# Folding the output weights over three steps of the attention instead of one, with the routed expert beats moved towards later steps

## The reference

```
q   = rmsnorm(rope(xn @ Wq_c @ Wq_up))            16 heads of 128
ao  = softmax(window scores, 64 keys) @ v + softmax(block scores, 16 blocks) @ ck
out = einsum('btgf,gfi->btgi', ao, Wg).reshape(...) @ Wo      4 groups of 4 heads
ffn = mean of 2 shared experts + sum over the top 6 of 32 routed experts
      of gate * (relu(xn @ w1 + b1) @ w2 + b2)
x   = x + out + ffn
```

## Time and profile before

| | |
|---|---|
| median of 3 runs | 601.38 us (600.21 to 603.71) |
| profiled execution | 597.51 us |
| its span | 595.7 us |
| busy TensorE, VectorE, ScalarE, GpSimd | 526.1, 335.0, 313.2, 328.8 us |
| steps -1 to 8 | from 83 us |

### The profile page before, as it was taken

One profiled execution on the slowest core, in us unless ns is written; L12 is line 12 of the kernel. 1 busy time (PEld: TensorE's weight loads), 2 busy tenths in 40 slices (PEclk: granted clock), 3 DMA queues, 4 the chain that ended last, 5 costly groups with the idle time before them and its releaser, 6 DMA issues.

```text
span 595.7 us, 9656 instructions
## 1 busy us (share of the span) xinstructions
PE 526.1 (88%) x2951; PEld 400.3 (67%) x2951; DVE 335.0 (56%) x884; ACT 313.2 (53%) x739; POOL 328.8 (55%) x235
## 2 busy tenths in 40 slices
PE   0998998799767999999999999999979997899982
PEld 0565786688666777788777887889757454455561
DVE  3479834233074471844818448251565986999654
ACT  1215136364556766767657676575621228667530
POOL 3000448868677685766867768654311024788770
PEclk9799998899899999999999999999999999999998
DMA  9940639778978886575765757865377012456667
GB/s 285 364 166 6 164 88 216 187 154 206 282 173 224 205 215 139 127 157 123 157 163 111 168 129 156 178 147 104 36 240 237 0 33 65 70 95 90 96 91 223
DMA packets 87281, 90.39 MB, mean 152 GB/s; under 512 B 26688, under 2 KB 75264, under 8 KB 86848
## 3 DMA queue, kind: packets, MB, share of 16 engines
q1 hardware_dynamic: 66608, 61.50, 35.4%
q0 software_dynamic: 19584, 27.24, 26.7%
q10 hardware_dynamic: 1040, 1.05, 0.5%
HBM read 65.32 MB, written 22.60 MB: 148 GB/s over the span
## 4 chain that ended last, share of the span: by engine, by line
PE 48%; DVE 16%; issue 12%; DMA 9%; ACT 7%; POOL 7%; SPq 0%; POOLq 0%; ACTq 0%; DVEq 0%
PE bank L559 9%; DMA expert_sums<-expert_weights,token_of_slot 7%; PE bank L896 6%; PE bank L904 3%; PE bank L905 3%; POOL tiles L1098 3%; PE bank L551 2%; PE bank L523 2%; PE bank L1804 2%; DVE sum_squares L686 2%; PE bank L568 2%; PE bank L491 2%; PE bank L511 2%; ACT normed L607 2%; POOL expert_weights L858 2%
## 5 line engine op out<-in xcount | busy, mean ns | idle before, releaser
L866 POOL DMA_INDIRECT expert_sums<-expert_weights,token_of_slot x79 | 128.8, 1631 | 55.2 <-ACT expert_weights L928 37.9
L858 POOL DMA_INDIRECT expert_weights<-normed_x,token_of_slot x79 | 94.5, 1196 | 109.2 <-DVE token_of_slot L366 45.6
L896 PE MATMUL bank<-expert_weights 128*88 128x128 f32 x632 | 85.3, 278 | 0.6 <-ACT expert_weights L921 0.4
L896 PEld LDWEIGHTS bank<-expert_weights 128*88 128x88 f32 x632 | 75.7, 161 | 1.2 <-issue 1.2
L559 PE MATMUL bank<-out_weights,expert_weights 128*128 128x256 f32 x256 | 60.1, 380 | 1.4 <-ACT expert_weights L644 1.4
L928 ACT ACTIVATE expert_weights<-bank,chosen_bf 128x256 f32<-128x256 f32 x79 | 37.7, 477 | 38.1 <-PE bank L905 18.9
L1105 POOL DMA_INDIRECT expert_sums<-expert_weights,token_of_slot x23 | 46.5, 2021 | 13.6 <-issue 5.5
L904 PE MATMUL bank<-expert_weights 88*128 88x256 f32 x158 | 48.6, 389 | 5.6 <-ACT expert_weights L928 5.5
L559 PEld LDWEIGHTS bank<-out_weights,expert_weights 128*128 128x128 f32 x256 | 46.4, 190 | 8.2 <-ACT expert_weights L644 3.1
L719 DVE SCALAR_TENSOR_TENSOR expert_weights<-bank,blocks_valid 128x64 f32<-128x64 f32 x32 | 7.1, 222 | 73.8 <-ACT expert_weights L621 73.8
L905 PE MATMUL bank<-expert_weights 89*128 89x256 f32 x158 | 47.6, 382 | 0.0
(11 more groups left out here) (276 smaller groups left out, 1087.5 us busy)
## 6 DMA issues: line engine op xcount, KB each, us to landing
expert_weights<-experts_out SPq DMA_DIRECT2D x79, 192.8 KB, 2.9
expert_weights<-experts_in SPq DMA_DIRECT2D x79, 176.0 KB, 3.2
expert_weights<-L_ffn_wi SPq DMA_DIRECT2D x32, 128.0 KB
expert_weights<-w_comp SPq DMA_DIRECT2D x1, 2048.0 KB, 9.1
expert_weights<-fold_g SPq DMA_DIRECT2D x1, 2048.0 KB, 13.8
expert_sums<-zeros SPq DMA_DIRECT2D x2, 1024.0 KB, 18.7
expert_weights<-L_ffn_wo SPq DMA_DIRECT2D x16, 128.0 KB
normed<-expert_sums SPq DMA_DIRECT2D x2, 1024.0 KB, 5.7
```

The source lines that it names most:

```text
L858: nc.gpsimd.indirect_dma_start(xt0[g % 4], None, xn0, bass.IndirectOffsetOnAxis(ap=MAP[:, g:g + 1], axis=0)).then_inc(gathered[g % 4], 16)
L866: nc.gpsimd.indirect_dma_start(sums0[g % 2], bass.IndirectOffsetOnAxis(ap=MAP[:, g:g + 1], axis=0), yt0[g % 2], None, compute_op=ALU.add). ...
L896: ins = nc.tensor.matmul(ps[5][0:DHB, c * P:(c + 1) * P], w[:, k * DH + c * DHB:k * DH + (c + 1) * DHB], xT0[g % NXT][:, k * P:(k + 1) * P ...
```

## The change

The tables of beats and folds are new: the beats per slot in steps -1 and 0 are thinned to 4 and 6, in steps 2 to 7 there are two beats in slot s = 0; the eight folds have their places in steps -1 (four), 0 (two) and 1 (two). The transfers of the values of batches 2 and 3 stand four beats earlier in SyncE's loop. The number of beats and folds and the work in each are the same.

```
-BEATS = {g: (1,) * 8 for g in range(FIRST_STEP, NT)}
-BEATS[NT] = (1,) * 7 + (0,)
+BEATS = {-1: (0, 1, 0, 1, 1, 0, 1, 0), 0: (1, 1, 0, 1, 1, 0, 1, 1), 1: (1,) * 8, **{g: (1, 1, 1, 1, 2, 1, 1, 1) for g in range(2, NT)},
+         NT: (1,) * 7 + (0,)}
+FOLDS = {(-1, 1): 0, (-1, 3): 1, (-1, 4): 2, (-1, 6): 3, (0, 4): 4, (0, 6): 5, (1, 4): 6, (1, 6): 7}
...
@@ attention_pe, and the same in attention_act with take_folded
-                if g == 0:
-                    fold(pe, k)
+                if (g, k) in FOLDS:
+                    fold(pe, FOLDS[g, k])
...
-                if g == 0:
-                    fold(pe, NG + s)
+                if (g, NG + s) in FOLDS:
+                    fold(pe, FOLDS[g, NG + s])
...
@@ SyncE's loop over beats
-                    if i == 48:
+                    if i == 44:
                         sp.wait_ge(pv_ps, NWIN)
-                    if 48 <= i < 49 + NWIN:
-                        load_values(sp, 2, i - 48)
-                    if i == 64:
+                    if 44 <= i < 45 + NWIN:
+                        load_values(sp, 2, i - 44)
+                    if i == 60:
                         sp.wait_ge(pv_ps, 2 * NWIN)
...
-                    if 64 <= i < 65 + NWIN:
-                        load_values(sp, 3, i - 64)
+                    if 60 <= i < 61 + NWIN:
+                        load_values(sp, 3, i - 60)
```

More of the change, by code:

```diff
@@ L662, in attention_act @@
                     probs_T(act, g - 2, 0)
-                if g == 0:
-                    take_folded(act, k)
+                if (g, k) in FOLDS:
+                    take_folded(act, FOLDS[g, k])
             for s in range(NSUB):
@@ L671, in attention_act @@
                         probs_T(act, g - 2, s + 1)
-                if g == 0:
-                    take_folded(act, NG + s)
+                if (g, NG + s) in FOLDS:
+                    take_folded(act, FOLDS[g, NG + s])
                 for i in beats(g, NG + s):
```

## The result

Over 19 runs of each the changed kernel takes 606.03 us (603.78 to 609.34) and the kernel before 603.49 (599.78 to 608.23). The ratio is 1.0047, with a 95% interval of 1.0028 to 1.0066: about 2.8 us slower, where 7.4 us faster was forecast. Some 2.9 us of the 8.5 arise ahead of step -1, where both kernels run the same code: beat 4 starts at 85.89 and not at 82.97, and in the ten traces of the experiments it starts at 84.95 to 86.48. The rest, 5.5 us, lies between there and step 8. The runs differ by 2.5 to 2.8 us, so about half of the 5.5 may be scatter between two single executions, and what follows places the loss within some 3 us. All lines of the changed kernel are one higher (L929 for L928).

A forecast was written before the change was run, and what follows sets the result against it. TensorE bounds step 3 and later ones like it; earlier, GpSimd and the two-tile output ring cannot follow close beats. Terms -6.2 + 0 - 1.2 = -7.4 us on 597.5 give 590.1; forecast's own range 589 to 597, whole range 583 to 602.

The forecast's parts named there:

- the ring: Two output tiles: ScalarE may evacuate tile g+2 only once tile g's scatter-add has landed, 4.95 us from scatter to evacuation.
- Steps -1 to 1, 6.2 us forecast: Early steps: losses beyond pure work fall from 25.7 to 19.5 us, 16 of waits and 3.5 of clock.
- The replay: Hand replay of the code order from 83 us: waits 4.6 us at beat 10, 5.2 at beat 15; 16 us lost.
- the 6.9 us of the prediction: Steps -1 to 1 before the change: at most this much lost to matmuls stretched by lowered clock after long gaps.
- Step 2, 0 forecast: Layout transfers entering its first half set against expert loads leaving it: 0, bounds -3 and +5 us.
- The burst: SyncE's layer-1 sums layout, two transfers of 1152 KB, moving from step 1's first half into step 2's.
- Steps 2 to 7, -1.2 forecast: Extra beat behind first scores: -0.6 us in each of six for L719's wait, GpSimd's delay against it.
- the ring's 0 to 0.8 us a step: Steps 2 to 7: GpSimd one tile later lengthens ScalarE's stall and delays the up-projection; 0.4 us taken.
- SyncE, 0 forecast: Transfers of batches 2 and 3's values issued four beats earlier, and its wait for all folds: nothing late, cost 0.
- The one by which the losses only move: Rival: early ring waits are replaced by those of beats 10, 15 and step 2; within 3 us; chance 0.16.
- the signs of being right: Step -1 no gap over 1 us; steps 0, 1 gaps 3-6; step 2 begins 160-166; steps 3-6 take 39-39.5 us.
- The slower rival: Rival: nine-beat steps 2 to 7 become bound by GpSimd, 6 us slower in sum, 607 us; chance 0.15.

The follow-up runs named there:

- Experiment 3: Changed kernel with the three transfers laying out layer 1's sums issued behind beats 55 to 57, not 22 to 24: 605.70 us, ratio 1.0038 to the kernel before.
- Experiment 4: Changed kernel with the extra beat of steps 2 to 7 one slot later, behind the second scores: 606.59 us, ratio 1.0055 to the kernel before.
- experiment 7: Changed kernel with three output tiles and the extra beat behind the second scores: 585.44 us, ratio 0.9716 to the kernel before.
- Experiments 2: Kernel before with the new table of beats alone, all eight folds in step 0: 601.46 us, ratio 0.9973 to the kernel before.
- 10: Changed kernel with all eight folds in step 0 and three output tiles: 586.99 us, ratio 0.9755 to the kernel before.
- 8: Changed kernel with six folds in step 0, two in step 1, none in step -1: 601.12 us, ratio 0.9979 to the kernel before.

## Why the prediction was wrong

**The bound.** That TensorE bounds the eight-beat steps from step 3 on, and the ring and GpSimd what lies ahead of them, held. Three tiles took 8.2 us from the kernel before and 12.7 from the changed one, which shows the ring directly.

**Steps -1 to 1, 6.2 us forecast, 3.9 measured.** The replay's two large waits came at the predicted beats and within 0.2 us of their size, and so did the shrinking one of 1.67 for L720 (1.3 forecast). What it had too small is the time after them, at the lower of the two clocks. First one of the four such stretches of the kernel before, then the two of the changed one:

```profile
112.90:116.20 3.30, 3.30 (x13) 2.72 (x12) 0.23 (x2) 0.45 (x2) 2.69 (x3) 0.53 1.04 229
```

```profile
113.40:120.00 6.60, 5.18 (x15) 3.39 (x16) 0.23 (x2) 4.63 (x12) 5.38 (x5) 0.52 0.75 147
137.40:147.40 10.00, 8.95 (x33) 6.89 (x34) 0.70 (x6) 5.51 (x15) 6.12 (x5) 0.52 0.63 121
```

The four of before are 3.3 to 3.8 us long each, with TensorE busy throughout, and took the 6.9 us of the prediction whole. The two of the changed kernel are 6.6 and 10.0 us long; TensorE is busy for 14.1 us of them, and 0.48 x 14.1 = 6.8 us went to the clock where I took 3.5. Two waits of 5 us thus cost as much clock as four shorter ones, and not half of it. The sum of these steps: of 21.8 us lost (82.9 less 61.1 of work) TensorE was idle for 13.4, 2.6 less than in the replay, the clock took 3.3 more than I gave it, and 1.6 us stand in neither, so 2.3 less were gained than forecast.

**Step 2, 0 forecast, 4.5 lost: the step that failed first.** The burst was weighed against the expert loads and set to nothing, with +5 as its bound; it is near the bound that it came. It was priced by the earlier trace rows at 6.04 - 4.95 us on a few scatters. The trace of before has a longer landing beside the same transfers (issued there at 150.52 and 158.08), 8.5 us, of which little was seen since TensorE itself came late in that stretch:

```profile
150.66 1.57 POOL L866 DMA_INDIRECT expert_sums<-expert_weights,token_of_slot  x1 [0.30 <-issue]
...
159.18 0.47 ACT L928 ACTIVATE expert_weights<-bank,chosen_bf 128x256 f32<-128x256 f32 x1 [2.29 <-issue]
```

In step 2 of the changed kernel the landing of 8.1 us met a TensorE that was not late, and became the wait of 5.88. Experiment 3 puts about 3.9 us of the step's loss on the layout transfers, a part of that by the clock, 0.92 in this step for 1.00 before. They also take part in step 3's loss: 2.1 of its 3.5 us went when they were moved. The waits of 1.58 and 1.42 us at 213.30 and 222.12 fell to one of 0.94 (at 209.69) by it. The wait at 222.12 follows a scatter that took 3.68 us to issue at 213.43 and held ScalarE until 221.11. VectorE ran L712 at that time:

```profile
213.38 2.28 DVE L712 TENSOR_TENSOR normed<-normed,rms 128x2048 f32<-128x2048 f32 x1
```

The Trainium skill (SBUF — State Buffer, "SBUF: two separate sides") has such a GpSimd operation blocked while VectorE holds the port pair that they share; this row agrees, as the earlier trace rows did: 3.68 us for a scatter whose neighbours take 1.58. No run here took L712 away, so that this is its cause was not shown. Of the 1.4 us of step 3's loss that stayed when the transfers were moved, the wait of 0.94 is a part; the rest was not placed.

**Steps 2 to 7, -1.2 forecast: wrong in sign.** Steps 4 to 7, clear of the burst, lost 1.4 us. The forecast rested on the wait for L719 falling from 0.94 to about 0.3. It is 0.98. I wrote that VectorE's chain comes later too and still took 0.6 off; its delay cancels the whole, since the chain of window norm and rotation starts with the second scores, which the extra beat delays by just its own length. Experiment 4 shows it: behind the second scores the same beat removes the wait. Its other half, the ring's 0 to 0.8 us a step, was in range: experiments 4 and 7 show that it stood right behind.

**SyncE, 0 forecast.** No wait for the values or for the folds stands in the trace. No run moved the values' transfers alone, so that they cost nothing was not shown beyond that.

**The rivals.** The one by which the losses only move came nearest, in number (within 3 us of before) and in mechanism: it named the waits of beats 10 and 15 and of step 2, and these are the 4.56, 5.38 and 5.88 us. I gave it 0.16. Of the signs of being right, those of steps -1 to 1 came; step 2 began at 168.80 and not by 166 (2.9 us of that ahead of step -1), and steps 4 to 6 took 39.7 to 40.2 us for 39 to 39.5.

The slower rival had the place right (nine-beat steps) and the mechanism wrong. It wanted GpSimd's rate to run out, with a stretch that grows; GpSimd's busy time in a step grew from 26.43 to 27.98, less than the 2.57 us of a gather and a scatter, and in experiment 7 it does the same work in 38.29 us. The limit was how long one scatter takes to land with two tiles in flight, not how many scatters fit. The rule of the Trainium skill named above, held to the letter for every VectorE operation with two inputs, finds little support in these busy times: nine tiles and the power alone take 9 x 2.57 + 3.2 = 26.3 us, so all of VectorE's 20.60 us of work in the step can have added 1.7 at most.

**What was not in the prediction at all** is that a fold in step -1 does harm. "Step -1 loses nothing: a fold stands near each beat" is true of TensorE and beside the point: GpSimd is by my own count the engine with the most to do up to step 1 (73.5 us, against 61.1 of TensorE's work; the trace has it busy for 58.5 us there, without the 0.30 us between its transfers), and folds between its first beats were idle time for it. I used that count against a rival only. Experiments 2 and 10 agree with this reading; that GpSimd's early idle time alone is the cause was not isolated, as no run fed it otherwise.

## What to carry to other kernels

Even out an overloaded stretch by the engine that limits it, not by the engine that is easiest to count: here, with the beats thinned out, filler work on TensorE between the first beats that feed GpSimd cost 4 to 6 us against the same work behind them (experiments 2, 8 and 10). Before moving work to cover a wait, ask from which event the waiting chain starts; in steps 2 to 7 filler ahead of that event delayed both and covered nothing. Price a transfer by the longest landing that stands beside it in the trace, also where nobody happened to wait for it. When two edits each bring next to nothing in a stretch, and each removes the wait it was aimed at, try them together: here a nine-beat step of 40.14 us took 39.98 with the later slot, 39.67 with a third tile and 38.29 with both.

## What the runs showed of the hardware

A scatter-add of 128 rows of 1 KB released its waiter 4.7 us after its start in quiet stretches (109.47 to 114.20) and 8.1 us after it while two transfers of 1152 KB ran (170.54 to 178.66). In experiment 3, with these transfers elsewhere, the same tile's scatter took 5.2 us (171.45 to 176.64), and the one that they then met 8.1. A third tile in flight, which gives a scatter one tile more to land, took 8.2 us from the kernel before and 12.7 from the changed one.
